# Softplus in one ScalarE pass from the bank, without a sum on GpSimd, and a new order of jobs

## What is computed

```
x     = silu(conv(x_in) + conv_b)
delta = softplus(x @ W_delta_1 @ W_delta_2 + b_delta_2)
A     = -exp(A_log)
h     = h * exp(delta * A) + (delta * x) * B      # for each token, 1024 channels, 16 states
y     = sum over states of h * C
out   = resid + ((y + x * W_D) * silu(skip)) @ W_out
```

## Time and profile before

| what | value |
|---|---|
| device time, median of 3 runs | 2828.54 us (2826.59 to 2828.7) |
| the profiled execution | 2828.89 us, of which the span of its instructions 2827.1 us |
| PE busy | 2625.4 us, 93% |
| DVE busy | 2464.6 us, 87% |
| POOL busy | 2391.6 us, 85% |
| ACT busy | 1878.3 us, 66% |
| granted TensorE clock, loop | 1.00 |
| chain that ended last, by engine | POOL 44%, PE 28%, issue 12%, DVE 7% |

### The profile page before, as it was taken

The page is one execution under the profiler, slowest core; times in us unless marked ns, Lnnn a source line. Parts: engine busy times, 40 slices in busy tenths (PEclk is TensorE's granted clock), DMA queues, the critical chain, the costliest instruction groups (busy, mean ns, idle before and its releaser), DMA issues.

```text
span 2827.1 us, 51682 instructions
## 1 busy us (share of the span) xinstructions
PE 2625.4 (93%) x17415; PEld 2029.6 (72%) x17415; DVE 2464.6 (87%) x3218; ACT 1878.3 (66%) x4340; POOL 2391.6 (85%) x2029
## 2 busy tenths in 40 slices
PE   5777899999999999999999999999999999998868
PEld 4565677777878777786777778687777778776635
DVE  6478899999999999999999989998999999898872
ACT  6374767676676767667676776667676766767541
POOL 1158899999898999999898999989999899999781
PEclk9888899999999999999999999999999999999889
DMA  7012223223222322222222222322222222222220
GB/s 271 30 55 64 59 65 76 54 61 79 62 72 60 80 50 70 70 62 72 64 74 61 75 62 58 77 60 71 59 78 58 61 74 66 72 59 76 48 69 16
DMA packets 95311, 194.41 MB, mean 69 GB/s; under 512 B 12685, under 2 KB 32713, under 8 KB 94537
## 3 DMA queue, kind: packets, MB, share of 16 engines
q0 software_dynamic: 20736, 75.51, 13.8%
q1 hardware_dynamic: 74312, 115.60, 13.0%
HBM read 106.66 MB, written 8.91 MB: 41 GB/s over the span
## 4 chain that ended last, share of the span: by engine, by line
POOL 44%; PE 28%; issue 12%; DVE 7%; ACT 2%; DMA 1%; POOLq 1%; DVEq 0%; ACTq 0%
POOL h L778 25%; PE ps L1597 9%; POOL h L795 7%; PE ps L1608 5%; POOL hl L884 5%; PE ps L1620 5%; PE ps L1554 3%; DVE h L1343 3%; PE ps L1669 3%; POOL delta L849 2%; POOL u L892 2%; DVE xc L1401 1%; PE ps L1630 1%; POOL h L784 1%; DMA xw<-h 1%
## 5 line engine op out<-in xcount | busy, mean ns | idle before, releaser
L778 POOL TENSOR_TENSOR h<-u,bb 128x1024 f32<-128x1024 f32 x512 | 1258.4, 2468 | 33.2 <-DVE u L1418 15.4
L1343 DVE TENSOR_TENSOR_SCAN h<-ps,h 128x512 f32<-128x512 f32 x1024 | 1191.2, 1206 | 51.1 <-POOL h L784 28.3
L1037 ACT ACTIVATE ps<-delta,a_neg 128x255 f32<-128x255 f32 x2048 | 873.0, 468 | 388.3 <-DVE h L1343 386.2
L1597 PE MATMUL ps<-xh,q_up 128*128 128x256 f16 x2048 | 467.3, 275 | 31.9 <-DVE xl L1280 19.0
L1597 PE MATMUL ps<-xh,q_gate 128*128 128x256 f16 x2048 | 465.5, 274 | 13.7 <-DVE xw L1434 13.3
L1365 DVE SCALAR_TENSOR_TENSOR y<-ps,ccur,y 128x512 f32<-128x512 f32 x672 | 466.8, 736 | 7.2 <-PE ps L1554 6.4
L1597 PE MATMUL ps<-xl,q_up 128*128 128x256 f16 x2048 | 467.1, 275 | 0.0
L1597 PE MATMUL ps<-xl,q_gate 128*128 128x256 f16 x2048 | 465.5, 274 | 0.0
L1554 PE MATMUL ps<-ident,h 128*128 128x128 f32 x2944 | 397.3, 278 | 63.5 <-DVE y L1365 59.4
L1554 PEld LDWEIGHTS ps<-ident,h 128*128 128x128 f32 x2944 | 344.2, 143 | 126.2 <-DVE h L1343 59.1
L884 POOL TENSOR_TENSOR hl<-act,hh 128x512 f16<-128x512 f32 x256 | 314.9, 1230 | 102.2 <-ACT hh L1064 99.6
(11 more groups left out here) (127 smaller groups left out, 3677.2 us busy)
## 6 DMA issues: line engine op xcount, KB each, us to landing
xw<-h POOLq DMA_DIRECT2D x144, 512.0 KB, 4.5
bb<-b_scratch SPq DMA_DIRECT2D x224, 256.0 KB, 3.1
cplane<-c_scratch SPq DMA_DIRECT2D x144, 128.0 KB, 3.1
xs<-in_L_attn_resid_dram SPq DMA_DIRECT2D x17, 512.0 KB, 3.6
out_dram<-xs SPq DMA_DIRECT2D x15, 512.0 KB, 4.3
wraw<-in_L_ffn_W_up_dram SPq DMA_DIRECT2D x4, 1024.0 KB, 9.6
wraw<-in_L_ffn_W_gate_dram SPq DMA_DIRECT2D x4, 1024.0 KB, 12.3
wraw<-in_L_ffn_W_down_dram SPq DMA_DIRECT2D x4, 1024.0 KB, 14.1
```

The lines of the kernel that those rows point to most:

```text
L778: ins = pl.tensor_tensor(hs, u[:, :, :], bb[:, q % 2, s % PLANES:s % PLANES + 1, :].broadcast_to([P, HE, CH]), ALU.mult)
L1037: ins = ac.activation(abar[r][:, e, 1:], delta[:, k, 1:], ACT.Exp, scale=a_neg[:, k, n:n + 1])
L1343: v.tensor_tensor_scan(hr, abar[r].rearrange("p e t -> p (e t)"), hr, 0.0, ALU.mult, ALU.add).then_inc(scanned, 1)
L1597: ins = te.matmul(pp[:, f * CH:(f + 1) * CH], w[:, d, col:col + P], part[:, d, :], start=(d == 0 and part is xh), stop=(d == DB - 1 and pa ...
```

## The change

Softplus becomes ACT's own function. When both banks of a half are due, ACT reads the four blocks from them with `ACT.Softplus` and the bias, straight into delta; the passes over tmp, the exponential, the logarithm and the sum on POOL (in the fill on DVE) are gone. Who waited for `delta_ready` now waits for the two banks' `bank_used`. `rms_scaled` waits for `xc_ready` instead. Beside it the slots of the loop, the lists of early and late work, `XD_0`, `XD_1`, `NEXT_LN` and `ELEM` are changed; `FIRST_SLOTS` and the other slot lists are the same. The counts of matmuls (15750 in the program) and of table loads (65) stay.

```diff
 LOOP_SLOTS = [
-    ["T1_1", "T1_0", ("OM_0", 0, 4)],
-    ["U1_0", "G1_0", "U1_1", "G1_1"],
+    ["T1_1", "T1_0", ("OM_0", 0, 3)],
+    ["U1_0", "G1_0", "U1_1", ("OM_0", 3, 4), "G1_1"],
...
-    ["G1_2", "D2_2", "U1_3"],
+    ["G1_2", "U1_3", "D2_2"],
     ["D2_3", "G1_3", "YT_2"],
...
-XD_0 = 0
-XD_1 = 9
+XD_0 = 1
+XD_1 = 6
...
-NEXT_LN = 29
+NEXT_LN = 30
-ELEM = [3, 9, 11, 15, 17, 18, 22, 27, 31]
+ELEM = [2, 9, 11, 15, 17, 18, 21, 27, 31]
...
+def delta_of(c, half):
+
+    if half:
+        return phase_of(c), c
+    return ("fill" if c == 0 else phase_of(c - 1)), c - 1
...
+        def need_delta(eng, c, half):
+
+            for q in (2 * half, 2 * half + 1):
+                bk, before = job_no(*delta_of(c, half), f"D2_{q}")
+                need(eng, bank_used[bk], before + 1)
...
-            def softplus(c, half):
-
-                need(pool, sp_step, 4 * c + 2 * half + 2)
-                dd = delta[:, half * HE:(half + 1) * HE, :]
-                pl.tensor_tensor(dd, dd, tmp_h, ALU.add).then_inc(delta_ready, 1)
...
-            def softplus_in(ph, i, q):
-
-                bk, pp = ready(ph, i, f"D2_{q}")
-                if q == 2:
-                    need(sc, abar_ready, 2 * STEPS * i)
-                    need(sc, u_ready, 2 * i)
-                    need(sc, delta_ready, 2 * i + 1)
-                for e in range(2):
-                    b, k = 2 * q + e, 2 * (q % 2) + e
-                    ac.activation(delta[:, b, :], pp[:, e * CH:(e + 1) * CH], ACT.Relu, bias=b2[:, b:b + 1])
-                    ins = ac.activation(tmp_h[:, k, :], pp[:, e * CH:(e + 1) * CH], ACT.Abs, bias=b2[:, b:b + 1])
-                ins.then_inc(bank_used[bk], 1)
...
-                ac.activation(tmp_h, tmp_h, ACT.Exp, scale=-1.0).then_inc(sp_step, 1)
-                need(sc, sp_step, 4 * c + 2 * half + 1)
-                ac.activation(tmp_h, tmp_h, ACT.Ln, bias=1.0).then_inc(sp_step, 1)
+            def softplus(ph, i, half):
+
+                c = i + 1 - half
+                need(sc, u_ready, 2 * c - 1 + half)
+                for q in (2 * half, 2 * half + 1):
+                    bk, pp = ready(ph, i, f"D2_{q}")
+                    for e in range(2):
+                        b = 2 * q + e
+                        ins = ac.activation(delta[:, b, :], pp[:, e * CH:(e + 1) * CH], ACT.Softplus, bias=b2[:, b:b + 1])
+                    ins.then_inc(bank_used[bk], 1)
...
-                need(sc, delta_ready, 2 * i + 2)
+                need(sc, xc_ready, 2 * i + 2)
...
-                    elif name[:2] == "D2":
-                        softplus_in(ph, i, int(name[3]))
+                    elif name in ("D2_1", "D2_3"):
+                        softplus(ph, i, int(name[3]) // 2)
...
-                v.tensor_tensor(dd, dd, tmp_h, ALU.add).then_inc(delta_ready, 1)
-                ve.wait_ge(delta_ready, 1)
                 v.tensor_tensor(u[:, :, :], dd, xc[:, 0:HE, :], ALU.mult).then_inc(u_ready, 1)
```

More of the change, by code:

```diff
@@ L98 @@
 LOOP_SLOTS = [
-    ["T1_1", "T1_0", ("OM_0", 0, 4)],
-    ["U1_0", "G1_0", "U1_1", "G1_1"],
+    ["T1_1", "T1_0", ("OM_0", 0, 3)],
+    ["U1_0", "G1_0", "U1_1", ("OM_0", 3, 4), "G1_1"],
     ["U1_2"],
-    ["G1_2", "D2_2", "U1_3"],
+    ["G1_2", "U1_3", "D2_2"],
     ["D2_3", "G1_3", "YT_2"],
     ["YT_3", "U1_4", "G1_4"],
[L105 to L110, removed]
+    ["U1_5", ("OM_0", 4, 6), "G1_5"],
+    ["U1_6", "G1_6", ("OM_0", 6, 7), ("DN1_0", 0, 3), ("OM_0", 7, 8)],
+    [("OM_1", 0, 1)],
+    [("OM_1", 1, 2), ("DN1_1", 0, 2), "U1_7", ("OM_1", 2, 6)],
+    [("OM_1", 6, 7), ("DN1_0", 3, 4), "G1_7"],
+    [("DN1_0", 4, 9), ("OM_1", 7, 8)],
     [("DN1_1", 2, 8), ("DN1_0", 9, 16)],
[L112 to L115, removed]
+    [("DN1_1", 8, 16)],
+    ["T2_1", "T2_0", ("SK_0", 0, 2)],
+    [("SK_1", 0, 2)],
+    [("SK_2", 0, 1)],
     [("SK_2", 1, 2), ("SK_3", 0, 2), "Tp_1", "Tp_0"],
-    ["G2_0", ("IN_2", 0, 2)],
+    ["U2_0", "G2_0", ("IN_2", 0, 2)],
     ["U2_1", ("IN_3", 0, 2)],
@@ L120 @@
     ["YT_1", "U2_2"],
[L121 to L124, removed]
+    ["G2_2", ("IN_1", 0, 1)],
+    [("IN_1", 1, 2), "U2_3", "G2_3", "U2_4"],
+    ["G2_4", ("DN2_0", 0, 3), "U2_5"],
+    ["G2_5", ("DN2_0", 3, 5), "DB"],
     [("DN2_0", 5, 7), "DT", "U2_6"],
-    ["D2_0", "G2_6", "D2_1"],
+    ["G2_6", "D2_0", "D2_1"],
     ["U2_7", ("DN2_0", 7, 8), "G2_7"],
@@ L578, in macaron_kernel @@
         ctanh_ready, xc_ready, xw_ready = sem("ctanh_ready"), sem("xc_ready"), sem("xw_ready")
-        sp_step, delta_ready, u_ready = sem("sp_step"), sem("delta_ready"), sem("u_ready")
+        u_ready = sem("u_ready")
         gtanh_ready, z_ready = sem("gtanh_ready"), sem("z_ready")
@@ L888, in u_of @@
                 need(pool, ub_ready, STEPS * c + half * N)
-                need(pool, delta_ready, 2 * c + half + 1)
+                need_delta(pool, c, half)
                 need(pool, xc_ready, 2 * c + turn(half) + 1)
@@ L931, in run @@
                         rms(ph, i)
-                    if ph != "fill" and after(ph, "D2_1", 2, s):
-                        softplus(i + 1, 0)
                     if ph != "fill" and after(ph, "D2_1", 3, s):
                         first_state(i + 1, 0)
-                    if after(ph, "D2_3", 2, s):
-                        softplus(i, 1)
                     if after(ph, "D2_3", 3, s):
@@ L1031, in exps @@
                 if s % N == 0:
-                    need(sc, delta_ready, 2 * i + half + 1)
+                    need_delta(sc, i, half)
                 for r in range(2):
@@ L1048, in first_decay @@
                     return
-                need(sc, delta_ready, 2 * c + half + 1)
+                need_delta(sc, c, half)
                 for e in range(HE):
@@ L1226, in run @@
                         hidden_high(ph, i, kind, p)
-                    if after(ph, "D2_1", ph != "fill", s):
-                        softplus_log(ph, i, i + 1, 0)
                     if ph != "fill" and after(ph, "D2_1", 2, s):
                         first_decay(i + 1, 0)
-                    if after(ph, "D2_3", 1, s):
-                        softplus_log(ph, i, i, 1)
                     if after(ph, "D2_3", 2, s):
```

19 lines of the change are left out of this document (8 added, 11 removed).

## The result

The changed kernel takes 2837.8 us (median of 5 runs, 2836.3 to 2839.6), the kernel before 2828.5 us: a ratio of 1.0036 with an interval of 1.0024 to 1.0048. It is slower by 9.3 us, where 34 us less was predicted. The profiled execution, one of the five, took 2839.6 us; the span of its instructions is 2837.8 us, 10.7 us more than before.

A forecast was written before the change was run, and what follows sets the result against it. POOL and PE were taken to bound the loop together. Loop 14 x (1.0 + 1.2) = 31, fill 4.8, first chunk -3.5, last 1.5 made 34 us: 2829 - 34 = 2795 us, range 2764 to 2831 us.

The forecast's parts named there:

- PE's need and the limits: Loop: PE needs 157.4 us of a 162.8 us round, leaving 5.4 us unused; POOL and PE bound it together.
- POOL's relief, 1.0 us a round: Loop: dropping Softplus's sum on POOL (4.7 us a round) gains 1.0 us a round, bounds 0 and 4.7.
- The rounds that begin a sequence and the others: Sign of being right: these two kinds of round closer than 1.3 us, since POOL no longer bounds either.
- ACT and the plan, +1.2 us a round: Loop: less ACT work and new slots shrink PE's holes, gaining 1.2 us a round, a quarter of what is left.
- Rival A: Only POOL's relief counts, ACT's and the plan's give nothing: 17 us gained, 2812 us; chance 0.20.
- Rival D: Slower: in the loop PE waits for D2_2's bank, held behind a table load ahead of YT_2: 2843 us; chance 0.12.
- the exponentials behind this block wait too: Second part of rival D, loop: exponentials wait 4.1 us in one piece; an earlier 4.7 us piece was held against it.
- The fill, -4.8 us: Fill: first u near 149.5 us instead of 154.42, a gain of 4.8 us, 3.4 if Softplus takes double.
- The first chunk, +3.5 us: First chunk: G1_1 waits for D2_2's bank and exponentials come later; net loss 3.5 us, bounds 0 and 7.
- near 181: First chunk: the next exponentials come near 181 instead of 174.02 us, and the scan waits for them.
- the 2.52 us that DVE had waited at 187.42: First chunk: DVE's wait for the old 4.7 us piece of exponential, logarithm and loads, set against the loss.
- The last chunk, -1.5 us: Last chunk: one sum fewer in a stretch that is POOL's chain, gain 1.5 us (0 to 2.4).

The follow-up runs named there:

- small_sum: The kernel before with POOL adding Softplus's parts (L849) for one token in 256, the other 255 sums left out: 2813.5 us, ratio 0.9947.
- d2_moved: old_plan with D2_2 behind U1_3 and D2_0 behind G2_6, each one job later: 2836.2 us, ratio 1.0026 against the kernel before.
- exp_ln: The kernel before, own plan, with Softplus as exponential passes from the banks and one logarithm a slot later, no sum on POOL: 2807.5 us, ratio 0.9928.
- exp_ln_d2: exp_ln with the two moves of d2_moved (D2_2 behind U1_3, D2_0 behind G2_6): 2810.4 us, ratio 0.9942 against the kernel before.
- old_plan: The changed kernel's native Softplus with the loop's slots and the early and late lists of the kernel before: 2868.8 us, ratio 1.0144.
- late_block: The changed kernel with D2_3's Softplus block behind its slot's exponentials in the loop's rounds: 2893.8 us, ratio 1.0234 against the kernel before.
- exp_ln_block: exp_ln with the logarithm pulled forward directly behind the passes of D2_1 and D2_3: 2890.7 us, ratio 1.0226 against the kernel before.
- no_loads: The changed kernel with Relu in place of Softplus, leaving out 64 of 65 table loads: 2819.8 us, ratio 0.9971 against the kernel before.

## Why the prediction was wrong, point by point

**PE's need and the limits: right.** The matmuls are the same in every run, so I keep the 157.4 us of need; what a round takes above it are holes: 5.8 us after, 5.4 before.

**POOL's relief, 1.0 us a round: right.** small_sum measured 0.85 us a round and 14.7 us of span in all. The rounds that begin a sequence and the others did come closer than 1.3 us: 488.48 / 3 = 162.8 and 163.3 us, 0.5 apart. But this is no sign that the reason was right: the short rounds became 1.1 us longer and the others 0.3, and the new wait for xw stands in both.

**ACT and the plan, +1.2 us a round: the step that failed.** Forecast were 2.2 us less a round, 1.0 of POOL and 1.2 of this; measured are 0.44 more. I took a quarter of the holes that were left, with no row behind that share, because ACT was "late" somewhere, and because most jobs keep their slots. In fact 19 of the 32 slot lists differ, and by d2_moved against after the plan beyond its two moves brings 0.26 us a round. By exp_ln against small_sum the relief is worth 0.0 us a round, with 4.6 us less of ACT's work (the change took 6.8; the other 2.2 weren't tested alone). What counted was not how much ACT does but where one uninterrupted piece of it stands. The block of 4.2 us costs 1.3 us a round (d2_moved against exp_ln_d2), more than POOL's relief brings. The table's rounds add up: 162.76, less 0.85 for POOL (small_sum), 0.0 for ACT (exp_ln), plus 0.25 for the two moves (exp_ln_d2), plus 1.29 for the block (d2_moved), less 0.26 for the rest of the plan are the 163.20 us of after. Rival A had the relief right and didn't price the block either.

**Rival D: the right place, dismissed by a wrong comparison.** D had two mechanisms. The held bank (its main one) is shown in old_plan and in late_block, and its estimate of 1.3 us to spare stands beside 0.8 us measured in after; after's plan keeps just clear of it. The other, "the exponentials behind this block wait too", I set aside, since a piece of 4.7 us was there before. That was the error. The old piece was as long and had the scan's exponentials behind it too, but it stood one slot further on, where DVE's wait reaches no bank that PE is about to open. The new one stands in the slot whose y + x frees the bank for G1_4, and there PE was late already: 0.4 us for xw in the earlier trace rows, so this handover had no slack at all. The order's rows of the first place showed which slot it was. exp_ln and exp_ln_block show the difference with the same instructions at two places: 161.9 and 167.7 us a round. The length of a piece says nothing without who waits behind it. D's price of 2843 us was nearer to the 2837.8 than the forecast, in part for another reason than its first.

**The fill, -4.8 us: right, a little more.** 5.8 us were gained at the first u; the other 1.6 us of that stretch's 7.4 came behind it. The rows that answer:

```profile
145.61 1.28 ACT L1117 ACT_TABLE_LOAD   x1
146.90 1.56 ACT L1117 ACTIVATE delta<-ps,vcol 128x256 f32<-128x256 f32 x4
...
148.58 1.23 DVE L1404 TENSOR_TENSOR u<-delta,xc 128x1024 f32<-128x1024 f32 x1 [11.07 <-ACT delta L1117]
```

u starts at 148.58 us (predicted 149.5, before 154.42), since the load (from 145.61) ran ahead of the bank rather than behind it.

**The first chunk, +3.5 us: mis-sized, it was +12.6.** The rows that answer:

```profile
166.77 0.37 PE L1583 MATMUL ps<-xh,q_gate 128*128 128x256 f16 x1 [6.29 <-ACT delta L1117]
...
175.74 1.65 ACT L1040 ACTIVATE ps<-delta,a_neg 128x255 f32<-128x255 f32 x4
...
187.67 1.45 POOL L891 TENSOR_TENSOR hl<-act,hh 128x512 f16<-128x512 f32 x1
189.15 0.69 ACT L1062 ACTIVATE act<-ps,tanh_sc 128x512 f32<-128x512 f32 x1 [6.94 <-POOL hl L891]
189.87 0.69 DVE L1361 SCALAR_TENSOR_TENSOR act<-act,ps 128x512 f32<-128x512 f32 x1 [3.98 <-ACT act L1062]
...
194.32 1.94 PE L1540 MATMUL ps<-ident,h 128*128 128x128 f32 x8 [6.37 <-DVE y L1353]
```

The first stall is as predicted: exponentials "near 181" in before's clock, 176.2 with the fill's 4.8 us taken off, 175.74 measured. What failed is the catching up behind it. I counted as a credit the 2.52 us that DVE had waited at 187.42 for the old piece. That piece is gone, but the tanh it delayed needs POOL's hl too, and in the new lists hl stands behind one more product of POOL: it runs at 187.67 us rather than 184.50. ACT is idle for 6.94 us, DVE waits 3.98, more than the 2.52 before, and PE waits 6.37. From there the scan is mostly 2 to 3 us behind before, and at the start of the loop it is 5.2. exp_ln, with the lists of before, takes 4.8 us of gain in the fill and shortens the first chunk by 3.6 us. The loads are 3.6 of the 12.6 us (no_loads); d2_moved, with the native blocks and the lists of before, has 5.8 of them. The other 6.8 come with the new plan; which of its lists does it wasn't separated.

**The last chunk, -1.5 us: not there.** The rest took 219.7 us in both, and small_sum took 219.0: POOL's relief alone is worth 0.7 us there, and what took that back in the changed kernel wasn't traced.
